# A decoder layer with a sparse expert block: the last layer norm is moved into the expert tiles

## The reference, cut to what matters

```
x = layernorm(x + self_attention(x))        # 16 heads of 16, 1024 keys
x = layernorm(x + cross_attention(x, ctx))  # one head, 77 keys
gate = softmax(x @ gate_w + gate_b)         # 8 experts
topv, topi = top_k(gate, 2);  topv = topv / topv.sum()
for each expert e:                          # only the two chosen ones count
    y_e = relu(x @ w1[e] + b1[e]) @ w2[e] + b2[e]      # 256 -> 1024 -> 256
x = layernorm(x + sum of topv * y_e over the two experts)
```

## Time and profile before

| | us |
|---|---|
| median of three runs | 1474.02 (1472.77 to 1474.66) |
| the profiled execution | 1476.74 |
| its span, first to last instruction | 1474.9 |
| TensorE busy in the span | 1406.7 (95%) |
| VectorE busy | 974.4 (66%) |
| POOL busy | 392.7 (27%) |
| the last TensorE product ends at | 1434.7 |

### The profile page before, as it was taken

One profiled execution on the slowest core, in us unless ns is written; L12 is line 12 of the kernel. 1 busy time (PEld: TensorE's weight loads), 2 busy tenths in 40 slices (PEclk: granted clock), 3 DMA queues, 4 the chain that ended last, 5 costly groups with the idle time before them and its releaser, 6 DMA issues.

```text
span 1474.9 us, 47861 instructions
## 1 busy us (share of the span) xinstructions
PE 1406.7 (95%) x18586; PEld 928.3 (63%) x18586; DVE 974.4 (66%) x1685; ACT 860.8 (58%) x1966; POOL 392.7 (27%) x676
## 2 busy tenths in 40 slices
PE   7999999999999999999999999999999999999990
PEld 3354445444444545444444458889999999999980
DVE  6777788888888888888988954656333333333326
ACT  3477788887777777778878783333333333333320
POOL 1211121212212215321225211455422222222223
PEclk9799999999999999999999999999999999999995
DMA  4324232334434323322433242224322222222216
GB/s 159 95 70 137 67 92 89 109 115 135 129 98 133 113 81 113 105 80 74 133 92 106 77 166 65 66 78 105 78 37 37 37 37 37 38 37 41 40 19 232
DMA packets 104840, 130.99 MB, mean 89 GB/s; under 512 B 25770, under 2 KB 81370, under 8 KB 103594
## 3 DMA queue, kind: packets, MB, share of 16 engines
q1 hardware_dynamic: 89322, 103.74, 23.3%
q0 software_dynamic: 14000, 19.48, 7.4%
q10 hardware_dynamic: 1296, 4.72, 0.8%
HBM read 75.98 MB, written 51.90 MB: 87 GB/s over the span
## 4 chain that ended last, share of the span: by engine, by line
PE 84%; DVE 8%; issue 3%; DMA 2%; ACT 1%; SPq 1%; POOL 0%; DVEq 0%; POOLq 0%; ACTq 0%
PE pa L1116 17%; PE pb L1130 16%; PE pa L893 14%; PE pb L893 13%; PE po L1063 13%; PE px L893 7%; DVE neg L1405 4%; PE px L886 2%; PE po L992 1%; ACT w_sb L1219 1%; PE px L967 1%; PE px L942 1%; DVE w_sb L1864 1%; DMA x<-space,y_tags 1%; SPq L477 0%
## 5 line engine op out<-in xcount | busy, mean ns | idle before, releaser
L1219 ACT ACTIVATE w_sb<-pb 128x512 f32<-128x512 f32 x996 | 590.0, 599 | 137.7 <-PE pb L893 102.8
L1405 DVE TENSOR_REDUCE neg<-pa 128x1 f32<-128x1024 f32 x512 | 612.0, 1213 | 87.2 <-PE pa L893 80.0
L893 PE MATMUL pb<-w_sb 99*32 99x512 bf16 x3984 | 393.4, 381 | 6.0 <-DMA w_sb<-minus_maxima 3.1
L1335 ACT ACTIVATE space<-pa,b1T_sb 128x128 f32<-128x128 f32 x568 | 154.7, 383 | 318.4 <-PE pa L1116 318.4
L893 PE MATMUL pa<-w_sb 96*32 96x512 bf16 (+1 forms) x4208 | 328.1, 385 | 11.6 <-DVE neg L1405 10.9
L1063 PE MATMUL po<-w_sb,space 128*32 128x256 f32 x4000 | 304.6, 379 | 0.0
L1116 PE MATMUL pa<-xgT,attn_t 128*128 128x128 f32 x2272 | 268.9, 275 | 0.4 <-DVE attn_t L1717 0.4
L1116 PEld LDWEIGHTS pa<-xgT,attn_t 128*128 128x128 f32 x2272 | 266.1, 192 | 4.9 <-issue 1.4
L1130 PE MATMUL pb<-w_sb,space 128*128 x1136 | 260.4, 380 | 0.0
L1130 PEld LDWEIGHTS pb<-w_sb,space 128*128 128x128 f32 x1136 | 208.8, 190 | 25.2 <-issue 0.3
L844 POOL DMA_INDIRECT x<-space,y_tags x71 | 116.9, 1647 | 366.8 <-DVE space L1782 299.5
(11 more groups left out here) (226 smaller groups left out, 973.9 us busy)
## 6 DMA issues: line engine op xcount, KB each, us to landing
xg<-x_by_expert SPq DMA_DIRECT2D x71, 130.0 KB, 2.5
w_sb<-w SPq DMA_DIRECT2D x17, 512.0 KB, 5.3
attention_out<-space SPq DMA_DIRECT2D x64, 128.0 KB, 2.1
w_sb<-w SPq DMA_DIRECT2D x7, 1024.0 KB, 8.0
q_parts<-w_sb SPq DMA_DIRECT2D x48, 128.0 KB
w_sb<-q_parts SPq DMA_DIRECT2D x64, 96.0 KB, 2.6
w_sb<-k_parts SPq DMA_DIRECT2D x64, 96.0 KB, 2.7
k_parts<-w_sb SPq DMA_DIRECT2D x45, 128.0 KB
```

The lines of the kernel that those rows point to most:

```text
L893: mm = pe.matmul(out[at:end], lhsT[:, at:end], rhs, start=start, stop=stop, tile_position=(0, at))
L1219: act.activation(ex_of(n)[:, half * HALF:(half + 1) * HALF], score_bank(n, half), ACT.Exp, scale=SCALE).then_inc(e_done, 1)
L1335: ins = act.activation(hT[tile % 2][:, f, :], pH[tile % 2][:, f, :], ACT.Relu, bias=g.b1_sb[:, bass.ds(e * FT + f, 1)])
L1405: dve.tensor_reduce(neg[i % 2][:, t:t + 1], pa[n % 2][:, :], AX.X, ALU.max, negate=True).then_inc(max_done, 1)
```

## The change

Each token's two results now have a DRAM row each in a new tensor `y_parts` of 2 x 6016 rows (token n: row n for its first expert, row 6016 + n for its second). A row's tags are four numbers: the own row, the weight, the other expert's row for this token, and the token's number. `y_parts` is set to zero at the start by 14 DMAs of up to 896 rows. The expert tiles then do, for tile t:

- `scatter`: a plain indirect store of the weighted result to the own rows of `y_parts`;
- `gather`: an indirect load of the other rows into `x3`, issued after the scatter of tile t - 1 has landed. It finds the other result where it is written already, and zeros where it is not;
- `residual`, `measure_3`: `x3` + token + own result, and its statistics;
- `spread_3` on POOL, `norm_3` on VectorE;
- `scatter_out`: an indirect store of the normed rows to the output. A token's second visit comes later than its first, finds both results and writes over the row of the first.

The tensor with the tokens, its stores, the add in the DMA and everything after the last tile are gone. The output tensor has 1920 rows more, into which padding rows fall.

```diff
-    XS = 3
+    XS = 4
+    ZEROS = -(-YP_ROWS // (SPARE * P))
+    PAST = Y_ROWS
+    OWN, WEIGHT, OTHER, TOKEN = (slice(D + i, D + i + 1) for i in range(4))
...
                 def load_xg(tile):
                     row = number(sp, tile, 0)
                     if tile >= XS:
                         sp.wait_ge(kept, tile - XS + 1)
                         sp.wait_ge(turned_x, tile - XS + 1)
+                        sp.wait_ge(c_both, tile - XS + 1)
...
-                    if late_half and j >= 1:
-                        store_x2(j - 1)
                     if i == 4:
...
-                        for e in range(NE + SPARE):
-                            sp.dma_start(g.x2_dram[B * S + e * P:B * S + (e + 1) * P, :], spare_rows[:, 0, 0:D]
-                                         ).then_inc(dump_out, 16)
+                    if 0 <= i - 3 < ZEROS:
+                        rows = slice((i - 3) * SPARE * P, min((i - 2) * SPARE * P, YP_ROWS))
+                        n = (rows.stop - rows.start) // P
+                        sp.dma_start(g.y_dram[rows, :].rearrange("(k p) d -> p k d", p=P), spare_rows[:, 0:n, 0:D]
+                                     ).then_inc(zeros_in, 16)
...
-                for n in range(NG):
-                    settle(sp, g.settled_dma)
-                    sp.dma_start(xr[:, n * GT:(n + 1) * GT, :], rows_of(g.x2_dram, n)).then_inc(sums_in[n], 16)
...
+                def gather(tile):
+                    pool.wait_ge(kept, tile + 1)
                     if tile:
                         pool.wait_ge(y_out[(tile - 1) % TAGS], 16 * ((tile - 1) // TAGS + 1))
+                    if tile >= 2:
+                        pool.wait_ge(out_rows, 16 * (tile - 1))
                     settle(pool, settled_pool)
-                    pool.indirect_dma_start(g.x2_dram, bass.IndirectOffsetOnAxis(y_tag[tile % TAGS][:, 0:1], 0),
-                                            y[tile % 2], None, bounds_check=Y_ROWS - 1, compute_op=ALU.add
-                                            ).then_inc(y_out[tile % TAGS], 16)
+                    pool.indirect_dma_start(x3[tile % 2], None, g.y_dram,
+                                            bass.IndirectOffsetOnAxis(y_tag[tile % TAGS][:, 2:3], 0),
+                                            bounds_check=YP_ROWS - 1).then_inc(x3_in, 16)
+                def spread_3(tile):
+                    pool.wait_ge(c_aggr, tile + 1)
+                    pool.tensor_tensor(c_dev[:, :], c_mv[:, 1:2], eps[:, 0:1], ALU.add).then_inc(c_var, 1)
+                    pool.wait_ge(c_var, tile + 1)
+                    pool.tensor_tensor(c_rstd[:, :], c_dev[:, :], g.neg_half[:, 0:1], ALU.pow).then_inc(c_rstd_done, 1)
+                def scatter_out(tile):
+                    pool.wait_ge(c_normed, tile + 1)
+                    if tile:
+                        pool.wait_ge(out_rows, 16 * tile)
+                    settle(pool, settled_pool)
+                    pool.indirect_dma_start(g.out, bass.IndirectOffsetOnAxis(y_tag[tile % TAGS][:, 3:4], 0),
+                                            x3[tile % 2], None, bounds_check=Y_ROWS - 1).then_inc(out_rows, 16)
+                def scatter(tile):
+                    pool.wait_ge(result_done, tile + 1)
+                    settle(pool, settled_pool)
+                    pool.indirect_dma_start(g.y_dram, bass.IndirectOffsetOnAxis(y_tag[tile % TAGS][:, 0:1], 0),
+                                            y[tile % 2], None, bounds_check=YP_ROWS - 1).then_inc(y_out[tile % TAGS], 16)
...
+                    if tile:
+                        spread_3(tile - 1)
+                    if tile == 0:
+                        pool.wait_ge(zeros_in, 16 * ZEROS)
+                        pool.wait_ge(pv_done, PAIRS)
+                    gather(tile)
+                    if tile:
+                        scatter_out(tile - 1)
...
+                def residual(tile):
+                    dve.wait_ge(x3_in, 16 * (tile + 1))
+                    dve.tensor_tensor(x3[tile % 2], x3[tile % 2], xg[tile % XS][:, 0:D], ALU.add).then_inc(c_both, 1)
+                def measure_3(tile):
+                    z = x3[tile % 2]
+                    dve.wait_ge(result_done, tile + 1)
+                    dve.wait_ge(c_both, tile + 1)
+                    dve.tensor_tensor(z, z, y[tile % 2], ALU.add).then_inc(c_sum, 1)
+                    dve.wait_ge(c_sum, tile + 1)
+                    dve.bn_stats(c_stats[:, :], z).then_inc(c_stat, 1)
+                    dve.wait_ge(c_stat, tile + 1)
+                    settle(dve, g.settled)
+                    dve.bn_aggr(c_mv[:, :], c_stats[:, :]).then_inc(c_aggr, 1)
+                def norm_3(tile):
+                    z = x3[tile % 2]
+                    dve.wait_ge(c_rstd_done, tile + 1)
+                    dve.tensor_scalar(z, z, c_mv[:, 0:1], c_rstd[:, 0:1], ALU.subtract, ALU.mult).then_inc(c_normed, 1)
...
                     if tile + 2 < FFN_TILES:
                         copy_w1(tile + 2, 1, e)
+                    if tile:
+                        residual(tile - 1)
+                        measure_3(tile - 1)
...
+                    if tile:
+                        norm_3(tile - 1)
                 result(FFN_TILES - 1)
+                residual(FFN_TILES - 1)
+                measure_3(FFN_TILES - 1)
+                norm_3(FFN_TILES - 1)
```

More of the change, by code:

```diff
@@ L692, in _ @@
                             sp.wait_ge(pads_in, 16 * NE)
[L693 to L697 removed]
+                        load_xg(tile - 1 + XS)
                     if tile == TB + SHIFT + 3:
@@ L1551, in weights @@
                     tokens = g.col["token"].start + b * TB
-                    dve.tensor_scalar(pay[b % 2][:, :, D].bitcast(I32), g.step_c[:, tokens:tokens + TB], 0.0, None,
-                                      ALU.add).then_inc(route, 1)
-                    dve.tensor_copy(pay[b % 2][:, :, D + 1], first).then_inc(route, 1)
+                    token = g.step_c[:, tokens:tokens + TB].rearrange("p (t o) -> p t o", o=1)
+                    for at, row in ((OWN, 0), (OTHER, Y_ROWS), (TOKEN, 0)):
+                        dve.tensor_scalar(pay[b % 2][:, :, at].bitcast(I32), token, float(row), None, ALU.add).then_inc(route, 1)
+                    dve.tensor_copy(pay[b % 2][:, :, WEIGHT], first.rearrange("p (t o) -> p t o", o=1)).then_inc(route, 1)
                 def tabled_1(name):
@@ L1657, in pads @@
                     for e in range(NE):
-                        dve.tensor_scalar(pad_rows[e][:, D:D + 1].bitcast(I32), g.step_c[:, col + e:col + e + 1], 0.0, None, ALU.add)
+                        for at, row in ((OWN, 0), (OTHER, PAST), (TOKEN, 0)):
+                            dve.tensor_scalar(pad_rows[e][:, at].bitcast(I32), g.step_c[:, col + e:col + e + 1], float(row), None, ALU.add)
                     dve.tensor_tensor(full[:, :], g.run[:, :], g.step_c[:, g.col["region"]], ALU.add).then_inc(pads_set, 1)
@@ L1763, in _ @@
                         dve.wait_ge(spare_set, 1)
-                        dve.tensor_copy(spare_rows[:, :, D].bitcast(I32), g.step_c[:, g.col["pads"]][:, NE:NE + SPARE]
-                                        ).then_inc(spare_set, 1)
+                        spare = g.step_c[:, g.col["pads"]][:, NE:NE + SPARE].rearrange("p (k o) -> p k o", o=1)
+                        for at, row in ((OWN, 0), (OTHER, PAST), (TOKEN, 0)):
+                            dve.tensor_scalar(spare_rows[:, :, at].bitcast(I32), spare, float(row), None, ALU.add).then_inc(spare_set, 1)
                 def keep(tile):
```

125 lines of the change are left out of this document (44 added, 81 removed).

## The result

| | before | changed |
|---|---|---|
| runs, median (lowest to highest) | 1473.59 us (1472.77 to 1474.66, 4 runs) | 1458.93 us (1458.42 to 1459.59, 4 runs) |
| ratio | | 0.9903, 95% interval 0.9888 to 0.9918 |
| profiled execution, its span | 1476.74, 1474.9 us | 1459.59, 1457.3 us |
| TensorE, VectorE, POOL busy | 1406.7, 974.4, 392.7 us | 1409.0, 1080.8, 556.7 us |

The change makes the kernel faster by 14.7 us by the medians and by 17.6 in the span. I had forecast 25.5. The range of 1441 to 1462 holds the time, but the forecast is 10.4 us too low, and the likeliest case had only 1442 to 1454. (Of the 10.4 us, 7.9 are missing from the gain in the span. The other 2.5 are my baseline: the profiled execution of before lies further above its median than that of the changed kernel.)

A forecast was written before the change was run, and what follows sets the result against it. TensorE was taken to bound the kernel up to 1434.7 us, followed by a 40.2 us tail. The terms -28.6 - 2.2 + 0 + 5.3 = -25.5 took 1474.0 to 1448.5 us, with 1441 to 1462 holding 8 in 10.

The forecast's parts named there:

- Step 1: After the last product: the 40.2 us tail goes, the last tile's own 11.6 us way out replaces it; -28.6 us.
- Step 2: SP's round 4 in the attention stage: without fifteen zero stores, TensorE no longer waits for the maxima; -2.2 us.
- Step 3: Steady expert tiles: added VectorE and POOL work fits into the 7.25 us of TensorE; 0 us.
- rival B: Early and middle tiles: POOL sets the pace, indirect DMAs taking 1.55 us or more whatever the add; 1459 us, chance 0.17.
- C: Expert tiles: the gather's round trip sets the pace from landings of 4.2 us on; at 5.2, 1518 us; chance 0.07.
- C2: Expert tiles: VectorE's copies lock POOL out, each indirect DMA taking 2.51 us; about 1604 us, chance 0.04.
- Step 4: Early and middle expert tiles: little idle time is left for the added VectorE and POOL work; +5.3 us.
- the round of positions: Early tiles, round after 917.5 to 929: new VectorE work counts in full, 2.4 us, and 0.5 in the round before.
- the 1.2 of the tiles 11 to 14: Around these tiles VectorE comes up to 5.8 us late against about 4.5 of slack; 1.2 us lost.
- my own signs of being wrong: Expert tiles: steady tile over 7.3 us, TensorE waiting for w1 copies beyond tile 15, or gathers landing late behind two stores.
- A: Whole kernel, likeliest case: the sum of the steps, 1448.5 us, with 1442 to 1454 about it; chance 0.62.
- the six cases: Whole kernel: the forecast's alternative outcomes, with chances 0.62, 0.17, 0.07, 0.04, 0.08 and 0.03.

The follow-up runs named there:

- e3: The changed kernel with the last tile's normed rows stored by SP as one plain block, once all other stores have landed; 1456.90 us.
- e7: The kernel before, with the 15 stores that clear the dump rows made as 3 of the same bytes; 1472.98 us.
- e1: The changed kernel with the residual sum taking the tile's own result in place of the token, so the token's buffer is free early; 1456.75 us.
- e5: The changed kernel with the 8 pad-row stores on SP spread over tiles 14 to 21, not in a row at tile 13; 1456.62 us.
- e2: The changed kernel without the output stores of the normed rows of tiles 10 to 21; 1455.51 us.
- e10: The changed kernel with the last batch's expert stores spaced over tiles 12 to 21 and the pad stores spread over tiles 14 to 21; 1455.72 us, ratio 0.9874.
- e4: The kernel before, with one more indirect store by POOL after the last norm and a wait for its landing; 1478.82 us.
- e12: The changed kernel with each tile's two expert stores on POOL moved behind the store of the normed rows; 1489.34 us.
- e9: The changed kernel with the last batch's 16 expert stores issued by POOL over ten tiles (2, 1, 2, 1, 2 a tile), not eight; 1456.33 us.

## Why the prediction was right or wrong

**Step 1, the tail: right up to the last store, 5.0 us short behind it.** The chain of `residual`, `measure_3`, `spread_3`, `norm_3` and the store came as laid out, 8.8 us for 8.7. The term "2.7 to landing: 1446.1, and about 0.2 to the end" is the one that was mis-sized: from the store's start to the end are 7.9 us. Behind the last packet stand 3.2 us in e3 and 3.3 in the kernel before, and in the changed kernel, with an indirect DMA by POOL as the last one, 2.7 more. The first part could have been read in the trace of before: its last packet lies 3.3 us ahead of the end. I had counted all 40.2 us as going away. The tail gave 23.4 in place of 28.6; its 16.8 us lie outside my bounds of 9.5 to 15.5, in which only landings were varied.

**Step 2, SP's round 4: right.** 2.36 us in the round for 2.2, TensorE busy for all of 126 to 140 us, and e7 has it alone. At the first tile 1.94 us are left, no more than executions differ by; the stores of zeros stayed hidden.

**Step 3, steady tiles: right.** 7.25 us each, TensorE busy for 324.00 of the 324 us from 1110 to 1434. Durations by line: the indirect DMAs take what the plain expert store did.

```profile
L859 POOL DMA_INDIRECT y_parts<-space,y_tags x71: 986/1001/1377, 898.5 to 1445.1; - x71
...
L837 POOL DMA_INDIRECT space<-y_parts,y_tags x71: 1081/1087/1390, 888.0 to 1442.4; - x71
...
L853 POOL DMA_INDIRECT out<-space,y_tags x71: 1025/1254/1504, 907.7 to 1449.4; - x71
```

The old scatter, with its add, took 0.55 us more (1551 against 1001 ns at the median). With that rival B, which gave the 1.55 us to the surroundings, has no ground, although POOL does set the pace of some middle tiles; C needed gathers that land in over 4.2 us, and the chain at the end shows 2.8 and 2.9; C2 needed 1.75 us for a DMA, and none of the 213 takes more than 1.50. The output store takes 1.25 us at the median, where 1.03 is the least. The Trainium skill (SBUF — State Buffer, "Who interferes with whom") has VectorE's two-port copies lock GpSimd out, and by that page's 3.1 us POOL would, as an estimate, have paced every tile. The trace shows nothing of that size; whether the output store's 0.2 us are this lock was not tried.

**Step 4, early and middle tiles: 5.3 forecast, 7.8 lost.** Up to the 15th tile it is 3.3 (the round of positions 2.2 for my 2.9, the rest in the two tiles around the first reweighting, which is three copies now and not one). From there on it is 4.45, where I had at most the 1.2 of the tiles 11 to 14, and this is the term that failed. I counted VectorE's lateness there and not POOL's sum: two expert stores, scatter, gather, output store and spread come to 7.81 us, over the tile's 7.25, for eight tiles in a row (to 9.1 in the one with the reweighting), by the very durations that I had in hand (5 x 1.3 + 1.1 = 7.6). I had summed POOL's round for the early tile (9.4 of 10.63) and the steady one (5.0 of 7.25), and not for the middle ones, where the round is short and the expert stores are still there. The second cause, the loads behind eight pad stores, I did not see: the pads come later and the loads have less of a lead. A token's buffer is now held until `residual` (with it free early, e1, no load is late), and with the pads spread (e5) none is late either.

The sum: 5.2 us of tail, 2.5 of tiles and 0.3 ahead of them are missing from the 25.5, which leaves 17.5; the span shows 17.6.

Of my own signs of being wrong one came: TensorE waits for w1 copies beyond tile 15 (twice from 1030 to 1110 us, as shown with e2). Three things that should have shown did not: 16.8 us from the last product to the end for 11 to 12, the last product at 1440.5 for 1437.8, and 2.0 of the 7.8 us in the tiles are lost behind 1040 us, where I had none. The time fell on rival B's 1459 and not into A's 1442 to 1454, and not for B's reason, which the durations rule out. That the range held is owed to B's middle having been taken in: luck in part. The chances of the six cases also add up to 1.01.

**A version that is probably ahead of both** is e10: 0.9874 (0.9855 to 0.9893) of the kernel before, where the change as it stands has 0.9903 (0.9888 to 0.9918). They were timed on different chips and the intervals overlap a little, so the times don't part the two. The tiles do in part, with 5.24 us lost for 7.76 in one execution each, where one total is uncertain by 1.5.

## What to carry to other kernels

Add up each engine's queue for every kind of round, above all for the short rounds in which extra work of another stage still runs: POOL had room in the early and in the steady tiles, and none in the eight between, least of all in the one with the reweighting. Work that stands ahead of a wait in a queue may be filling it for free: before moving it, look at what the engine would wait for without it. And when two things are late at the same place, taking one away shows the other; test them alone and together. Before you compare losses, look at the granted clock in the same stretch: behind a stall it can add nearly as much again as the stall.

## What the runs showed of the hardware

- A span ends 3.2 to 3.3 us after the last packet of a DMA from SyncE's or ScalarE's queue, and 5.4 to 7.6 after that of an indirect DMA by POOL (changed kernel 5.9, e10 5.4, e4 7.6; read in slices of 0.2 us).
- An indirect DMA of 128 rows of 1 KB occupies POOL for 1.00 us as a plain scatter, 1.09 as a gather, 1.03 to 1.25 as a scatter to the output, and 1.55 when it adds; each has some 0.3 us of issue ahead of it. Landing from the start, at the median: 2.5 us plain, 2.7 to the output, 2.9 for a gather (e12), 3.8 with the add.
- Fifteen stores of 0.13 MB hold SyncE's queue for 10.5 us; as three stores of the same bytes 4.2 us (e7), and TensorE has no wait there.
- Behind a wait of 2.0 us TensorE's granted clock was at its lower level, 0.50 in the profile's terms, for 3.4 us in e9, and a `down` took 5.33 us for 3.62; behind waits of 2.2 to 2.5 us in the changed kernel, e2 and e3 it stayed at 1.00.
- The start of the tiles, at some 890 us, moves by up to 6 us between executions whose code up to there is the same.
